# Content weights of the feed-forward branch: high and low halves side by side in one stationary matrix, two matmul passes instead of three

## The reference

```
spikes = sigmoid(xn @ enc_w + enc_b)                    # 512 -> 1024
cont   = spikes @ s2c_w + s2c_b                         # 1024 -> 64, the "content" of a token
rh     = relu(cont @ r_w1 + r_b1)                       # 64 -> 64, the router
probs  = softmax(rh @ r_w2 + r_b2)                      # 64 -> 8 experts, the best two are taken
eo     = experts 1 and 2 of the token applied to cont   # 64 -> 512 -> 64 each
out   += layernorm(sigmoid(sigmoid(mix @ c2s_w + c2s_b) @ dec_w + dec_b))
```

## Time and profile before

| | us |
|---|---|
| median of three runs (2024.8 to 2026.93) | 2026.44 |
| the profiled execution, its own time | 2028.13 |
| its span, first to last instruction | 2026.4 |
| PE busy | 1965.3 (97% of the span) |
| DVE busy | 1045.1 (52%) |
| ACT busy | 814.9 (40%) |
| POOL busy | 392.9 (19%) |
| stage A, PE's first encode matmul to stage B's first matmul | 18.1 to 523.65 |

### The profile page before, as it was taken

The page is one execution under the profiler, slowest core; times in us unless marked ns, Lnnn a source line. Parts: engine busy times, 40 slices in busy tenths (PEclk is TensorE's granted clock), DMA queues, the critical chain, the costliest instruction groups (busy, mean ns, idle before and its releaser), DMA issues. The chain is left out here.

```text
span 2026.4 us, 25149 instructions
## 1 busy us (share of the span) xinstructions
PE 1965.3 (97%) x9100; PEld 1609.1 (79%) x9100; DVE 1045.1 (52%) x1846; ACT 814.9 (40%) x1359; POOL 392.9 (19%) x428
## 2 busy tenths in 40 slices
PE   7999999999899999998899989999999999999998
PEld 5888888888788888887678768888888888888886
DVE  5445455553442222222888645555556556566554
ACT  4444445444221222112677533444344443444442
POOL 1000000000003444431000122222222222222220
PEclk9999999999999999999999989999999999999999
DMA  5561324423112233321877512222222222222210
GB/s 200 209 236 69 141 90 145 169 89 122 69 65 99 110 112 113 112 107 54 317 232 236 187 49 89 89 88 89 88 88 88 88 88 78 73 78 78 84 66 34
DMA packets 74826, 233.95 MB, mean 115 GB/s; under 512 B 9856, under 2 KB 15952, under 8 KB 68176
## 3 DMA queue, kind: packets, MB, share of 16 engines
q1 hardware_dynamic: 66432, 219.58, 30.7%
q0 software_dynamic: 8272, 12.76, 2.2%
HBM read 151.95 MB, written 80.36 MB: 115 GB/s over the span
## 5 line engine op out<-in xcount | busy, mean ns | idle before, releaser
L569 DVE TENSOR_TENSOR spl<-sp_t,sph 128x512 fp32r<-128x512 f32 x128 | 88.6, 692 | 240.1 <-ACT sph L391 240.1
L103 PE MATMUL A_E<-xs,enc_h 128*128 128x512 f32 x512 | 206.8, 404 | 0.0
L105 PE MATMUL A_E<-xs,enc_h 128*128 128x512 f32 x512 | 200.8, 392 | 0.0
L1574 DVE TENSOR_TENSOR ratel<-rate,rateh 128x512 fp32r<-128x512 f32 x128 | 88.5, 691 | 217.4 <-ACT rateh L1384 177.4
L104 PE MATMUL A_E<-xs,enc_l 128*128 128x512 f32 x512 | 200.6, 392 | 0.0
L1501 PE MATMUL D_D<-dec_h,rateh 128*128 128x512 f32 x512 | 199.8, 390 | 0.0
L1502 PE MATMUL D_D<-dec_l,rateh 128*128 128x512 f32 x512 | 199.8, 390 | 0.0
L1503 PE MATMUL D_D<-dec_h,ratel 128*128 128x512 f32 x512 | 199.5, 390 | 0.0
L1376 ACT ACTIVATE rate<-D_Y,cols 128x512 f32<-128x512 f32 x128 | 87.9, 687 | 264.3 <-PE D_Y L1453 261.5
L387 ACT ACTIVATE sp_t<-A_E,cols 128x512 f32<-128x512 f32 x128 | 88.1, 688 | 245.4 <-PE A_E L105 245.4
L863 POOL DMA_INDIRECT slots_scratch<-ctok,idx x128 | 123.8, 967 | 249.3 <-DVE v L991 123.4
(11 more groups left out here) (283 smaller groups left out, 4810.3 us busy)
## 6 DMA issues: line engine op xcount, KB each, us to landing
xs_scratch<-xs SPq DMA_DIRECT2D x16, 2048.0 KB, 9.3
xsd<-xs_scratch SPq DMA_DIRECT2D x16, 2048.0 KB
xs<-xs_scratch SPq DMA_DIRECT2D x14, 2048.0 KB, 8.5
wt<-ew_scratch SPq DMA_DIRECT2D x39, 513.0 KB, 3.8
x<-in_x SPq DMA_DIRECT2D x16, 1024.0 KB, 5.9
xd<-in_x SPq DMA_DIRECT2D x16, 1024.0 KB
out_y<-out SPq DMA_DIRECT2D x64, 256.0 KB, 2.1
slots_scratch<-zt SPq DMA_DIRECT2D x1, 9984.0 KB
```

What stands on the lines that cost most here:

```text
L103: pe.matmul(out, w_hi, x_hi, start=start, stop=False)
L105: return pe.matmul(out, w_hi, x_lo, start=False, stop=stop)
L569: dve.tensor_tensor(T["spl"][:, n % 3, :], T["sp_t"][:, m % 2, :], f32(T["sph"][:, n % 3, :]), ALU.subtract)\
L1574: dve.tensor_tensor(ratel[:, n % 3, :], rate[:, k % 2, :], f32(rateh[:, n % 3, :]), ALU.subtract)\
```

## The change

The stationary matrix of the content becomes one tensor `s2c` with the high half of the 64 columns in columns 0 to 63 and their low half in columns 64 to 127. Two matmuls a chunk, with `sph` and with `spl` moving, then give the content's high part in rows 0 to 63 of A_S and its low part in rows 64 to 127. The content is the sum of both halves of rows. Before, there were three matmuls a chunk.

Three places take up the sum. The router contracts all 128 rows with `r_w1` twice, as before, but now `r_w1` itself needs its own low half in a matrix of its own (`r1h`, `r1l`), so that the router has three matmuls instead of two. The content by token is made by a DVE reduction over the two halves, out of A_C into 64 columns of `ctok`; ACT then copies these into the other 64 columns, and waits for DVE to do so. The bias is added to rows 0 to 63 only. The sums for the bias take 8 small matmuls instead of 16.

```diff
@@ place
-    split("A", "s2c", [P, HC, P])
+    put("A", "s2c", [P, HC, P], F32R)
+    put("A", "s2c_raw", [P, HC, P])
@@
-    put("A", "r1", [P, P], F32R)
+    for n in ("r1h", "r1l"):
+        put("A", n, [P, P], F32R)
@@ ACT, router
-                act.wait_ge(S["ctr_done"], i + 1)
-                act.activation(T["ctok"][:, i * NT:(i + 1) * NT, :],
-                               bC[:, :].rearrange("p (t c) -> p t c", t=NT), ACT.Copy).then_inc(S["ctok_out"], 1)
+                act.wait_ge(S["ctok_out"], i + 1)
+                act.activation(T["ctok"][:, i * NT:(i + 1) * NT, MOE:P], T["ctok"][:, i * NT:(i + 1) * NT, 0:MOE],
+                               ACT.Copy).then_inc(S["ctok_twice"], 1)
@@ ACT, before the blocks
-            act.activation(T["s2c_h"][:, :, :], T["s2c_raw"][:, :, :], ACT.Copy).then_inc(S["wh_out"], 1)
+            act.activation(T["s2c"][:, :, 0:MOE], T["s2c_raw"][:, :, 0:MOE], ACT.Copy).then_inc(S["wh_out"], 1)
@@ PE, content
-                pass3(pe, bS[:, :], T["s2c_h"][:, m, :], T["s2c_l"][:, m, :], T["sph"][:, n % 3, :], T["spl"][:, n % 3, :],
-                      m == 0, m == HC - 1).then_inc(S["s2c_done"], 1)
+                pe.matmul(bS[:, :], T["s2c"][:, m, :], T["sph"][:, n % 3, :], start=(m == 0), stop=False)
+                pe.matmul(bS[:, :], T["s2c"][:, m, :], T["spl"][:, n % 3, :], start=False, stop=(m == HC - 1))\
+                    .then_inc(S["s2c_done"], 1)
@@ PE, router
-                pe.matmul(bR[:, :], T["r1"][:, :], T["conth"][:, :], start=True, stop=False)
-                pe.matmul(bR[:, :], T["r1"][:, :], T["contl"][:, :], start=False, stop=True).then_inc(S["rt1_done"], 1)
+                pass3(pe, bR[:, :], T["r1h"][:, :], T["r1l"][:, :], T["conth"][:, :], T["contl"][:, :], True, True)\
+                    .then_inc(S["rt1_done"], 1)
@@ PE, block 0, the weights' sums
-                            pe.matmul(bL[:, 0:2], T["s2c_h"][:, c, :], T["ones"][:, 0:2], start=(c == 0), stop=False)
-                            k = pe.matmul(bL[:, 0:2], T["s2c_l"][:, c, :], T["ones"][:, 0:2], start=False,
+                            k = pe.matmul(bL[:, 0:2], T["s2c"][:, c, :], T["ones"][:, 0:2], start=(c == 0),
                                           stop=(c == HC - 1))
@@ DVE, router, behind rhl
+                dve.wait_ge(S["ctr_done"], i + 1)
+                dve.tensor_reduce(T["ctok"][:, i * NT:(i + 1) * NT, 0:MOE],
+                                  bC[:, :].rearrange("p (t h c) -> p t c h", t=NT, h=2), AX.X, ALU.add)\
+                    .then_inc(S["ctok_out"], 1)
@@ DVE, before the blocks
-            dve.tensor_tensor(T["s2c_l"][:, :, :], T["s2c_raw"][:, :, :], f32(T["s2c_h"][:, :, :]), ALU.subtract)\
+            dve.tensor_tensor(T["s2c"][:, :, MOE:P], T["s2c_raw"][:, :, 0:MOE], f32(T["s2c"][:, :, 0:MOE]), ALU.subtract)\
                 .then_inc(S["wl_out"], 1)
@@ DVE, block 0
-                        dve.tensor_copy(T["r1"][:, :], r_w1).then_inc(S["prepared"], 1)
+                        dve.tensor_copy(T["r1h"][:, :], r_w1).then_inc(S["prepared"], 1)
...
-                        dve.tensor_tensor(T["r1"][MOE:P, :], r_w1[MOE:P, :], f32(T["r1"][MOE:P, :]), ALU.subtract)\
+                        dve.tensor_tensor(T["r1l"][:, :], r_w1, f32(T["r1h"][:, :]), ALU.subtract)\
                             .then_inc(S["prepared"], 1)
...
-                        dve.scalar_tensor_tensor(out=T["s2c_b"], in0=bL[:, 0:1], scalar=0.5, in1=T["s2c_b"],
-                                                 op0=ALU.mult, op1=ALU.add).then_inc(S["prepared"], 1)
+                        dve.scalar_tensor_tensor(out=T["s2c_b"][0:MOE, :], in0=bL[0:MOE, 0:1], scalar=0.5,
+                                                 in1=T["s2c_b"][0:MOE, :], op0=ALU.mult, op1=ALU.add)
+                        dve.tensor_scalar(T["s2c_b"][MOE:P, :], bL[MOE:P, 0:1], 0.5, None, ALU.mult)\
+                            .then_inc(S["prepared"], 1)
```

## The result

The changed kernel took 2006.55 us (median of 5 runs, 2004.78 to 2008.04) against 2026.93 us before (5 runs, 2024.8 to 2029.6). The ratio is 0.9898, 95% interval 0.9884 to 0.9911: 20.4 us faster, where 26.2 were forecast, and above the range that ended at 2003. The profiled execution took 2008.04 us, its span is 2006.3.

The account below looks back on a forecast made before the run. PE's instruction list was taken to bound stage A's steady blocks. Content -29.0, router +3.7, weight sums -0.85 and all else 0 gave -26.2 us, from 2026.44 to 2000.2 us; range 1997.5 to 2003.

Parts of the forecast that it names:

- What bounds the kernel: Steady blocks of stage A: PE's instruction list sets the 31.04 us, so a matmul taken out shortens the block.
- None recurs by block: PE's waits in stage A: few and single, 12.6 us at the start, 0.8 and 2.0 us in the tail.
- What a matmul is worth: Content and router matmuls in stage A: 0.23 us each, from distances between starts in the trace.
- the sums: Weight sums for the bias in block 0: eight of 16 small matmuls go, 0.106 us each, 0.85 us off.
- the sum itself: Whole kernel: content 29.0 us off, router 3.7 on, weight sums 0.85 off, other parts 0; net -26.2 us.
- A wait by block and starts that move apart: Signs of a wrong prediction: PE waiting every block for `sp_t`, `spl` or norm, or PE's starts spreading in shortened rounds.
- The granted clock: TensorE's clock at stage B's start, 0.50 after PE's tail waits: up to 1.6 us either way, taken as 0.
- the late transfer: Load of x behind the 10 MB zero-fill, used by statistics at 124.40: 0 to 2.3 us; 8% including small waits.
- The tail: Behind stage A's last encode: two removed matmuls gain nothing, `spl` wait grows 0.8 to 1.2 us, reduction and copy hidden.
- The content by token: DVE reduction (675 ns) and ACT copy (400 ns) each block: chunk 4's tanh 0.3 us late, 3.9 to spare, cost 0.
- the slower rival: Chunk 4's tanh behind ACT's copy delays chunk 6's encode if the reduction lasts over 4.6 us; 2%.
- The other prices of a matmul: Each net removed matmul worth 0.106 us (2013.9 us; 3%), 0.131 (2011.2) or the listed 398 ns (1981.8; 2%).

Follow-up runs that it names:

- fillers: 19 matmuls into an unread bank, in stage A's tail, added to the changed kernel and to its version with rounds of four: 1.6 and 1.75 us faster.
- the second profile of the changed kernel: The changed kernel run again, unaltered, beside three other kernels on the same chip: 21.9 us below the kernel before.

## Why the prediction was wrong

*What bounds the kernel* held in the main: PE's list of instructions sets the block, and no other engine took over. "None recurs by block", read from the waits of the kernel before, did not last: with the change one does. The rows read for it also leave out a third wait of the tail, 1.5 us for `rhl`, which hardly changed (1.4 after).

*What a matmul is worth* held for the matmuls taken out and put in: 28.88 us for the content against 29.0, 0.90 for the sums against 0.85. A router matmul costs 0.244 rather than 0.23. Most of that is not the content's doing: with three content matmuls in the changed kernel the router takes 697 ns, against 458 for the two matmuls before, 0.239 for the third; the other 0.006 come with rounds of two.

**The step that failed** is the sum itself: it charged the change only with the matmuls that it removes and adds, and put the 1536 encode matmuls at no change. They became 3.6 us slower, 28 ns a round of twelve. Two things are in this. The larger is their spacing, which the sum took as given. The smaller, 0.5 to 0.9 us, is a wait that it put at nothing: it followed the turn of chunk 3 and the tanh of chunk 4, but not the turn of chunk 7, whose low half had 0.11 us to spare before the change and lost 0.23. A wait by block and starts that move apart were both named as signs that the prediction is wrong, and both came. The kernels with one to five content matmuls a round, in the old layout and in the new, with and without the new work of DVE and ACT, show that the number of content matmuls brings both. The rows of before held a hint: 12 matmuls behind a content round took 2.73 us, 0.2275 each, while the content's own took 0.23 and more. A distance that depends on what stands ahead is no constant. Together with the router's 0.2 and the content's 0.1, stage A gave 22.2 us for 26.2.

*The granted clock* was named, bounded at 1.6 us each way and taken as 0. At the place it was named for, stage B's start, the profiled pair lost 0.6 us, inside the bound. As the whole price of that place 1.6 us is small: with fillers stage B takes 429.0 us, without them 430.6 and 431.7 in the two profiles. Stage C's 1.4 us lay outside what was bounded; the second profile of the changed kernel does not have them. The upper end of the range was built from the late transfer and not from this bound, which lies in every run. Even so stage A's 4.0 us alone would have gone past it. Whether the change itself lowers the mean clock (2.6 us by the line) or merely met it is not settled: no experiment moved stage B's start without altering the tail.

*The tail* came as worked out (0.8 to 1.2 us, reduction hidden). *The content by token*: reduction 0.683 us for 0.675, copy 0.42 for 0.40, ACT's chain 2 us later, tanh in time; the slower rival never got near its 4.6 us. *The late transfer* was real and free. DVE's timeline at the place named with the earlier trace rows:

```profile
118.69 0.69 DVE L571 TENSOR_TENSOR spl<-sp_t,sph 128x512 fp32r<-128x512 f32 x1 [1.31 <-ACT sph L393]
119.52 0.69 DVE L544 BATCH_NORM_STATS2 st<-x 128x6 f32<-128x512 f32 x1
```

The statistics start 0.83 us behind `spl` instead of the 0.61 of other blocks, just behind the landing of their load at 119.50: 0.2 us late, within DVE's idle time.

*The other prices of a matmul* are out: content rounds give 28.88/126 = 0.229 us each.

## What to carry to other kernels

When matmuls are taken out of a list that PE works through without a break, sum the distances of all its starts in the new trace, not only those of the matmuls that went: the neighbours' spacing can change with the length of a group. Read the waits of the weight loads as well: here a wait in every block stood there, while the matmuls were shown busy throughout. And before taking a matmul out, look at everything that another engine makes in its shadow: 0.11 us to spare was less than the 0.23 taken out. Short groups of other operands between long ones are worth putting together: here two rounds of two made into one of four brought the encode matmuls back to 358.6 us in all, from 362.3 (358.7 before the change). Where PE waits at a stage's end, look at the granted clock behind it, and put its whole price into the range.

## What the hardware showed that I had not expected

Encode matmuls of one form follow each other at 226 to 227 ns when undisturbed, and at 224 to 236 ns for up to nine distances behind a content round, in one series; rounds of 1, 2, 3, 4 and 5 content matmuls leave the following twelve at 2744, 2760, 2730, 2745 and 2734 ns. Encode behind encode into the other bank shows none of it. A weight load waited 0.21 us in every block while the profile showed PE busy for 29.67 of 29.67 us. With nineteen unread matmuls in PE's waits the medians are 1.6 and 1.75 us lower, about as much as the scatter of the runs.
